# A four-layer graph network on one core: counts issued by ScalarE, residual rows loaded earlier, one left-over step later

## The reference

```python
# layer 0:  Ax = adj @ h;  1 - 0.1 * h - 0.01 * sum(h * Ax, axis=1)
# layer 1:  two hops:  agg = adj @ y;  y = tanh(concat([agg, y]) @ W[k])
# layer 2 (the masked layer):
#   mask = adj != 0;  rank = cumsum(mask, axis=1);  deg = rank[:, -1:]
#   k = min(deg, 100);  pos = rank - (deg - k)
#   w = mask * where(pos > 0, 0.5 ** (k - pos), 0);  w @ (h @ weight) + bias
# layer 3:  tanh([h, t] @ W1 + b1) @ W2 + b2 + adj @ hB - rowsum(adj) * hB,   hB = h @ B.T
```

## Time and profile before

| | us |
|---|---|
| median of 3 runs | 733.83 (732.15 to 735.96) |
| the profiled execution | 736.61 |
| its span, first to last instruction | 734.8 |
| TensorE busy | 685.3 (93%) |
| VectorE busy | 463.5 (63%) |
| ScalarE busy | 192.0 (26%) |
| GpSimd busy | 113.6 (15%) |
| read from HBM | 254.38 MB, 354 GB/s over the span |

### The profile page before, as it was taken

One profiled execution on the slowest core, in us unless ns is written; L12 is line 12 of the kernel. 1 busy time (PEld: TensorE's weight loads), 2 busy tenths in 40 slices (PEclk: granted clock), 3 DMA queues, 4 the chain that ended last, 5 costly groups with the idle time before them and its releaser, 6 DMA issues.

```text
span 734.8 us, 10203 instructions
## 1 busy us (share of the span) xinstructions
PE 685.3 (93%) x3680; PEld 267.3 (36%) x3680; DVE 463.5 (63%) x797; ACT 192.0 (26%) x295; POOL 113.6 (15%) x132
## 2 busy tenths in 40 slices
PE   3999999999899999999999997898988899999997
PEld 1433333333233333334344433344444433333332
DVE  7677777677888888857666767888888830000000
ACT  2101111111111111110000103687888831111111
POOL 5011001111100000002222222311222121211111
PEclk9999999999999999999999999999999999999999
DMA  8999999995699999779999994799999849999994
GB/s 358 414 414 412 414 413 413 412 412 231 222 384 409 334 377 378 327 279 369 373 393 364 346 389 180 290 402 392 358 379 367 321 176 345 412 398 406 369 390 170
DMA packets 47522, 260.71 MB, mean 355 GB/s; under 512 B 6576, under 2 KB 16560, under 8 KB 17264
## 3 DMA queue, kind: packets, MB, share of 16 engines
q1 hardware_dynamic: 38640, 252.18, 87.3%
q10 hardware_dynamic: 8832, 7.87, 3.4%
HBM read 254.38 MB, written 5.64 MB: 354 GB/s over the span
## 4 chain that ended last, share of the span: by engine, by line
PE 55%; DMA 31%; DVE 8%; issue 2%; POOL 2%; ACT 1%; DVEq 0%; SPq 0%; ACTq 0%
PE accA L1262 40%; DMA land<-adj_blocks 27%; DVE uS L1053 3%; PE work L1297 3%; PE accA L1310 3%; DVE uS L1035 2%; DMA xin<-x_rows 2%; PE work L1280 2%; PE work L1131 1%; PE work L1171 1%; PE work L1225 1%; POOL rstd L683 1%; PE accA L1231 1%; PE work L1206 1%; DMA wS<-weights 1%
## 5 line engine op out<-in xcount | busy, mean ns | idle before, releaser
L1262 PE MATMUL accA<-land,X 128*64 128x512 f32 x1504 | 365.6, 601 | 22.7 <-DVE X L1092 11.2
L1262 PEld LDWEIGHTS accA<-land,X 128*64 128x64 f32 x1504 | 99.6, 137 | 198.2 <-issue 140.4
L1035 DVE TENSOR_TENSOR uS<-uS,land 128x512 f32<-128x512 f32 x186 | 132.7, 714 | 28.0 <-DMA land<-adj_blocks 19.6
L1053 DVE TENSOR_SCALAR uS<-land 128x1024 bf16<-128x1024 f32 (+1 forms) x188 | 129.2, 725 | 33.4 <-DMA land<-adj_blocks 32.0
L1262 PE MATMUL accA<-cache,X 128*64 128x512 f32 x544 | 133.8, 597 | 2.9 <-ACT accS L781 2.9
L537 ACT ACTIVATE wS<-work 128x1024 uint16<-128x1024 f32 x112 | 108.0, 1029 | 23.9 <-PE work L1297 23.2
L1297 PE MATMUL work<-uS,triA 128*128 128x512 bf16 x256 | 76.0, 379 | 14.7 <-DVE uS L1053 8.8
L690 POOL TENSOR_TENSOR hS<-tS 128x256 f32<-128x256 f32 x24 | 23.6, 982 | 372.9 <-DVE tS L898 372.9
L1019 DVE TENSOR_TENSOR tS<-uS,work 128x256 f32<-128x256 f32 x8 | 3.4, 422 | 121.8 <-PE work L1171 121.8
L1310 PE MATMUL accA<-wS,X 128*128 128x512 bf16 x256 | 75.8, 379 | 0.0
L1262 PEld LDWEIGHTS accA<-cache,X 128*64 128x64 f32 x544 | 39.4, 138 | 71.2 <-issue 60.7
(11 more groups left out here) (91 smaller groups left out, 393.1 us busy)
## 6 DMA issues: line engine op xcount, KB each, us to landing
land<-adj_blocks SPq DMA_DIRECT2D x219, 1024.0 KB, 8.1
cache<-adj_blocks SPq DMA_DIRECT2D x17, 1024.0 KB, 11.7
x_rows<-zS ACTq DMA_DIRECT2D x24, 128.0 KB, 7.3
xin<-x_rows ACTq DMA_DIRECT2D x24, 128.0 KB, 7.2
uS<-counts SPq DMA_DIRECT2D x64, 4.0 KB
out_rows<-zS ACTq DMA_DIRECT2D x8, 128.0 KB, 7.0
rows_transposed<-rowsT SPq DMA_DIRECT2D x7, 128.0 KB, 7.8
wS<-rows_transposed SPq DMA_DIRECT2D x7, 128.0 KB, 7.6
```

Of the source, the lines that this page charges most:

```text
L1035: nc.vector.tensor_tensor(total, total, of[:, i * W:(i + 1) * W], ALU.add)\
L1053: nc.vector.tensor_scalar(masks(b)[0:rows, :], block_of(p, c, b)[0:rows, :], 0.0, None, ALU.not_equal)\
L1262: last = nc.tensor.matmul(accA[k * D:(k + 1) * D, c % 2, :], tile(X[p % 2], TQ * q + k), of[:, k * W:(k + 1) * W], start=(b == 0), stop=(b ...
```

## The change

1. The counts of pairs 4 to 63 of L2 are issued by ScalarE: behind each odd block's `weights_out` it waits for the triangle product of that block's pair and issues the counts four pairs on. The counts of pairs 0 to 2 are issued by SP at the start of L1B's steps 5, 6 and 7, those of pair 3 at the start of L2, ahead of its loads.
2. The stage "rows" of L1B goes from block 1 of the next chunk's step (for the last chunk: ahead of L2's first block, behind stage 8) to block 12 of the same chunk's.
3. The stages "left" and "left out" of L0's last chunk go from block 15 of L1A's first chunk to blocks 5 and 7 of its second.

```diff
-AHEAD = 3
-STAGES_L1B = {"rows": 1, 1: 3, "added": 5, ...
+STAGES_L1B = {1: 3, "added": 5, ...
-               "stack": 14, "counts": 14, "weights": 14, "left": 15, "left out": 15},
+               "stack": 14, "counts": 14, "weights": 14},
+LEFT_L1A = {"left": 5, "left out": 7}
...
-        return found + at_block({"rows": ROWS_L2}, (p, c)) if p == L2 else found
+        return found + at_block({"rows": ROWS_AT}, (p, c)) if p in (L1B, L2) else found
...
     if p == L1B:
-        return at_block({8: 2}, before2) if before2 and b == 2 else at_block(STAGES_L1B, before)
+        found = at_block({8: 2}, before2) if before2 else []
+        return found + at_block(STAGES_L1B, before) + at_block({"rows": ROWS_AT}, (p, c))
...
+    if p == L1A and c == 1:
+        found += at_block(LEFT_L1A, (L0, NC - 1))
...
-        return [(8, before2), ("rows", before), (1, before)]
+        return [(8, before2), (1, before)]
...
             def counts_for(g):          # SP
-                if g < MASKS // 2:
-                    sp.wait_ge(sums_done, 2 * g + 2)
-                else:
-                    sp.wait_ge(tri_done, 2 * (g - MASKS // 2) + 2)
...
+                sp.wait_ge(sums_done, 2 * g + 2)
+                sp.dma_start(*counts_of(g)).then_inc(counts_in[g % (MASKS // 2)], 16)
...
-                for i in range(issued["counts"], min(g + AHEAD, PAIRS * NC - 1) + 1):
-                    counts_for(i)
-                    issued["counts"] = i + 1
...
             def step(p, c, before, before2):          # SP
+                if p == L1B and c >= NC - 3:
+                    if c == NC - 3:
+                        sp.wait_ge(counts_out, 16 * NC)
+                    counts_for(c - NC + 3)
                 if p == L2 and c == 0:
-                    sp.wait_ge(counts_out, 16 * NC)
                     sp.wait_ge(left_out, 16 * NC)
                     left_over(0)
                     left_over(1)
-                    after_masks(-1)
+                    counts_for(3)
...
             def main(p, c, b):          # ScalarE
                 if p == L2 and b not in evac_on_dve(c):
                     weights_out(act, nc.scalar, c, b)
+                if p == L2 and b % 2:
+                    counts_for((NQ * c + b) // 2 + MASKS // 2)
+
+            def counts_for(g):
+
+                if g < PAIRS * NC:
+                    act.wait_ge(tri_done, 2 * (g - MASKS // 2) + 2)
+                    act.dma_start(*counts_of(g)).then_inc(counts_in[g % (MASKS // 2)], 16)
```

More of the change, by code:

```diff
@@ L257 @@
 HT_ACT = {L0: "turned", L1A: "turned", L1B: "turned", L2: 7}
-ROWS_L2 = 12
+ROWS_AT = 12
 ROW_STAGES = {"rows": 4, "hidden": 2, "tanh0": 5, "tanh1": 6, "intra": 9}
@@ L265 @@
 STAGES_L2 = {0: 2, "join0": 4, "join1": 5, 4: 6, 5: 8, 6: 10, 7: 13, 8: 15}
-STAGES_L1B = {"rows": 1, 1: 3, "added": 5, "tanh": 6, 3: 7, 4: 8, 5: 10, "turn": 12, "turned": 13, 6: 15, 7: 15}
+STAGES_L1B = {1: 3, "added": 5, "tanh": 6, 3: 7, 4: 8, 5: 10, "turn": 12, "turned": 13, 6: 15, 7: 15}
 QUICK = {L1A: {0: 0, 1: 1, 3: 1, 4: 1, 5: 2, 6: 4, 7: 6, "turn": 10, "turned": 10, "hop": 11, "hopped": 12, "part": 13,
-               "stack": 14, "counts": 14, "weights": 14, "left": 15, "left out": 15},
+               "stack": 14, "counts": 14, "weights": 14},
          L1B: {1: 1, "added": 2, "tanh": 3, "turn": 5, "turned": 5, "hop": 7, "hopped": 8},
@@ L293, in stages_after @@
     found += at_block(stages, before) if before else []
-    return found + at_block({"rows": ROWS_L2}, (p, c)) if p == L2 else found
+    if p == L1A and c == 1:
+        found += at_block(LEFT_L1A, (L0, NC - 1))
+    return found + at_block({"rows": ROWS_AT}, (p, c)) if p == L2 else found
 def early_stages(p, c, before, before2):
     if p == L2 and c == 0:
-        return [(8, before2), ("rows", before), (1, before)]
+        return [(8, before2), (1, before)]
     return []
@@ L537, in weights_out, with counts_of @@
                 ops.activation(w, of, ACT.Relu).then_inc(w_ready, 1)
+        def counts_of(g):
+            c, k = g // PAIRS, pair_order(L2, g // PAIRS)[g % PAIRS]
+            at = (2 * g) % MASKS * BLK
+            return (uS[LAST:P, at:at + 2 * BLK].rearrange("o (t w) -> o t w", w=W),
+                    counts_d[ch(L2, c), 4 * k:4 * k + 4, :].rearrange("(o t) w -> o t w", o=1))
         block = ctx.enter_context(nc.Block())
@@ L609, in _ @@
             LEFT_ROWS_AT = {NC - 3: 1, NC - 2: 3, NC - 1: 7}
-            issued = {"keep": 0, "counts": 0, "left": 2, "left rows": NC - 3}
+            issued = {"keep": 0, "left": 2, "left rows": NC - 3}
             def step(p, c, before, before2):
+                if p == L1B and c >= NC - 3:
+                    if c == NC - 3:
+                        sp.wait_ge(counts_out, 16 * NC)
+                    counts_for(c - NC + 3)
                 if p == L2 and c == 0:
-                    sp.wait_ge(counts_out, 16 * NC)
                     sp.wait_ge(left_out, 16 * NC)
```

## The result

The changed kernel takes 729.30 us in the median of 9 runs (726.31 to 730.21), the one before 733.83 beside it: a ratio of 0.9932, 95% interval 0.9913 to 0.9951, 4.5 us less. Run again with the later experiments it gave 730.77, ratio 0.9935 [0.9911, 0.9959]. Forecast were 727.0 and a range of 720 to 733.5: faster, as forecast, by two thirds of the size.

The account below looks back on a forecast made before the run. In L2, loads and counts were taken to hold each other up, close above a DMA floor. Gains 3.8 + 0.2 + 2.3 + 0 + 0.5 = 6.8 us gave 727.0 against the median 733.83; range 720 to 733.5.

Parts of the forecast that it names:

- the rate: L2's DMA rate with SP's queue freed: 400 GB/s, between 383 and 416, so 16.9 us a chunk instead of 17.6.
- Step 1: L2 from its second chunk: counts issued by ScalarE land sooner, SP's loads go earlier; 3.8 us gained, bounds nothing to 7.2.
- Step 2: Residual's rows loaded a chunk sooner: VectorE's wait shrinks, 0.2 us within L1B and 2.3 at the change to L2.
- Steps 3 and 4: Counts 0 to 3 issued early around L2's start: 0; last left-over weights later in L1A: 0.5 us, between 0 and 1.35.
- (a): L2: DMA is the limit or the ring makes no difference; 17.6 us a chunk stays, 730.8 us in all; chance 0.20.
- (b): L2: counts never late, loads at 416 GB/s, 7.2 us gained there and 3 to 4 elsewhere; 723 us; chance 0.25.
- (c): L2 blocks 4 and 6: counts behind rows on ScalarE's ring land after 10 us; slower, 743 us; chance 0.08.
- (d): Change to L2: early rows land among full loads and do not help; 2.3 us less gain, 729.3; within the forecast's 0.47.

Follow-up runs that it names:

- half loads: Changed kernel, but from L2's second chunk each load fetches only the first block of its pair; 720.42 us, ratio 0.9830 to the kernel before.

## Why the prediction was right in the whole and wrong in its sizes

*The bound.* That the DMA is the limit of L2 and the counts a hold on it was right; half loads show the first, the counts alone the second. But of the two waits that were to be undone, SyncE's came back as a wait for masks (88.5 and 87.3 us). That the freed queue would lift the rate from 383 to 400 GB/s came less than half true: over 480 to 560 us it is 376 to 381 in six profiles without the counts' move, 384 to 394 in five with it (384 in the first of the changed kernel), 379 with the rows on SyncE's queue.

*Step 1, the counts, 3.8 us.* Its mechanism came in part as described: the counts land 1.9 us sooner, there is no stop at 10 and 12, and ScalarE's pace shows no cost. Block 14, which was to be free of its stop, is only shortened (1.94 to 1.60), and in the changed kernel block 6 behind the rows grows from 1.85 to 2.24 and block 0 from 1.41 to 2.00. Alone it brings 2.4 to 2.9 us. Chunks 2 to 7 of L2 sum up to 105.3 to 107.3 us in those six profiles (mean 106.0) and to 103.1 to 103.9 in the three of the changed and the counts-only kernel (103.6): 2.4 us. From the start of L2's last chunk to the end of the kernel the three then lose 2.3 us in the mean against the first profile of before, and those six, that profile included, 1.3. The mis-sized term is the rate.

*Step 2, the early rows, 0.2 in L1B and 2.3 at the change of layer.* This is the step that failed. It measured 4.5 us alone, and not at the change of layer (0.9 us with the last chunk's rows alone). The mistake: I priced the transfer by who waits for it (1.0 us within L1B, "mostly hidden") and took one execution's 2.55 for the kernel's. The price was not with those who wait for the transfer: TensorE's waits for the loads fall from 3.7 to 4.9 us to 1.4 to 2.2 where the rows are at block 12. From the start of L1B to that of L2, four other profiles with late rows lie -1.25 to +1.0 us from the first, the one with rows at block 14 (that long execution) +2.5, and seven with rows at block 12 -3.7 to -4.7. What it is in the old place that holds the loads stays open, as said above.

*Steps 3 and 4.* No cost of the early counts is to be seen: in the kernel with the counts alone the first chunk of L2 takes 18.0 us, as short as any. The left-over step measured 0.4 us (0.9994) with an interval from -1.1 to 2.0, so its 0.5 is neither shown nor refuted.

*The sum.* An overestimate of 1.4 us in the counts and 1.4 at the change of layer stands against 3.4 missed in L1B: these offset each other, and it is luck that they did; without the 3.4 the changed kernel would have been near 732.7, close to the slow end of the range. By its terms the forecast was less good than by its total. The parts measured alone give 7.1 and the whole 4.8 to 5.0. If that difference is real, the load-bound L2, where stops come back elsewhere, would explain it; this is argued from the tables, not shown by a run of its own.

*The rivals.* (a), that nothing comes in L2, gave 730.8, which is near the medians, but for a wrong reason: L2 gains and L1B makes up the rest. The rule of the Trainium skill behind it ("DMA: Bandwidth & Descriptors", section "Issuing engines are not separate DMA queues") would have had the counts land as late as before and left the rate as it was. On the rate the traces go against it only a little, 384 to 394 for 376 to 381 GB/s, and SyncE's freed queue can explain that within the rule. On lateness they go against it plainly: 4.7 us from issue to landing instead of 6.6, and for the last counts of a chunk 4.3 instead of 8.3 once the rows are on another ring. So a small transfer depends on what stands ahead of it on its own ring. (b) needed a rate of 416. (c), counts behind rows, happened at its place: they land after 8.3 us, just where (c) put the turn to a loss (8.2), and not 10; block 6 takes 0.4 us a chunk more than before, where (c) had a loss of 1.8. (d) was the opposite of what the rows did.

## What to carry to other kernels

Price a transfer that is moved by the loads it runs beside, not only by who waits for it: here the place of one 128 KB transfer, beside the store and late in the chunk or 7 us earlier, was worth about 4 us to the loads, and its late landing 0.9 us at most, within the noise. In a stretch that the loads bind, a stop taken away comes back at another block, so test the bound with half the bytes before tuning the order. And read a wait of 2 us that occurs once in a profile against a second profile of the same kernel before it becomes a term.

## What the runs showed of the hardware

A stop can cost more than itself. In the kernel with the rows at block 14 TensorE stood 2.28 us for a load until 420.69, and the granted clock was half of full speed (1.2 GHz) from 419.9 to 426.7; the next 8 matmuls, which take 1.9 us at the full clock (403.57 in the same trace), took 3.68 and the 8 after them 3.15. Below are the windows and the timeline's row. It does not follow every such stop: in the kernel with L2's rows on SyncE's queue TensorE stood 2.52 us until 495.0 and 2.22 us until 529.5 in L2, and the clock stayed at full speed.

```profile
419.00:422.00 3.00, 1.31 (x4) 0.53 (x6) 1.96 (x4) 0.42 (x1) 0.00 (x0) 0.65 1.00 420
422.00:425.00 3.00, 3.00 (x8) 0.71 (x6) 2.74 (x6) 0.00 (x0) 0.61 (x1) 0.50 0.73 306
425.00:428.00 3.00, 3.00 (x12) 0.90 (x10) 1.16 (x5) 0.00 (x0) 1.62 (x2) 0.72 0.88 317
...
420.69 3.68 PE L1263 MATMUL accA<-land,X 128*64 128x512 f32 x8 [2.28 <-DMA land<-adj_blocks]
```

A small transfer lands by what is ahead of it on its ring and by the loads beside it. The 4 KB of counts landed 6.6 us after their issue on SyncE's ring with the 1 MB loads, 4.7 on ScalarE's with 128 KB rows in it, 4.4 on ScalarE's without them, and 2.0 with the rows in it but half the bytes of the loads (medians, chunks 2 to 7 of L2).
